# Attention laid out pair by pair: the odd row block's scores ahead of both weighted sums, turns and the layer norm's root in one fixed order

## What is computed

```python
x = x + attn(layernorm(x), Wqkv, bqkv, Wo, bo)
x = x + ffn(layernorm(x), gate_w, up_w, down_w, fc1_w, fc2_w, expert_w, ln_gamma, ln_beta)
# attn: 2048 rows in each of two sequences
qkv = x @ Wqkv + bqkv
p = softmax(q @ k.T / 16)
out = (p @ v) @ Wo + bo
```

## Time and profile before

| | us |
|---|---|
| median of 3 runs | 2429.43 (2427.39 to 2431.49) |
| the profiled execution | 2431.42 |
| its span, first to last instruction | 2429.6 |
| TensorE busy | 2324.2 (96%) |
| VectorE busy | 1762.6 (73%) |
| GpSimd busy | 1570.8 (65%) |
| ScalarE busy | 903.7 (37%) |
| transfers of the one queue | 382.38 MB, 54.1% of 16 engines' span |

### The profile page before, as it was taken

One profiled execution on the slowest core, in us unless ns is written; L12 is line 12 of the kernel. 1 busy time (PEld: TensorE's weight loads), 2 busy tenths in 40 slices (PEclk: granted clock), 3 DMA queues, 4 the chain that ended last, 5 costly groups with the idle time before them and its releaser, 6 DMA issues.

```text
span 2429.6 us, 31320 instructions
## 1 busy us (share of the span) xinstructions
PE 2324.2 (96%) x11224; PEld 1937.7 (80%) x11224; DVE 1762.6 (73%) x2952; ACT 903.7 (37%) x1695; POOL 1570.8 (65%) x1185
## 2 busy tenths in 40 slices
PE   6999999998999899999999999999999999999996
PEld 5888888887888788878887887787788778788875
DVE  6889957777777542954689775478795468977869
ACT  3222233333333352444432443443254343244442
POOL 4466525564555677499757469856749975744584
PEclk8999999999999999999999999999999999999998
DMA  8899845669566843344436343635534543633452
GB/s 219 251 314 303 256 151 174 193 200 314 169 199 194 242 130 95 101 120 129 117 106 183 107 129 90 150 93 161 146 103 119 130 113 101 190 105 98 120 155 91
DMA packets 218970, 386.48 MB, mean 159 GB/s; under 512 B 19648, under 2 KB 99648, under 8 KB 218176
## 3 DMA queue, kind: packets, MB, share of 16 engines
q1 hardware_dynamic: 217664, 382.38, 54.1%
q10 hardware_dynamic: 1152, 2.10, 0.2%
HBM read 260.67 MB, written 90.18 MB: 144 GB/s over the span
## 4 chain that ended last, share of the span: by engine, by line
PE 63%; DVE 12%; POOL 12%; DMA 6%; issue 3%; SPq 3%; ACT 1%; DVEq 0%; POOLq 0%; ACTq 0%
PE ps L2215 21%; PE ps L2216 20%; PE ps L2217 20%; POOL hq L2044 3%; DMA pland<-pturn 2%; POOL wr1l L1962 2%; POOL wr2l L1962 2%; POOL wr0l L1962 2%; SPq L637 2%; DVE xi L1292 2%; POOL pt L1962 1%; DVE pturn L1354 1%; DVE xr L1616 1%; POOL xr L2051 1%; DMA stf<-ups 1%
## 5 line engine op out<-in xcount | busy, mean ns | idle before, releaser
L1962 POOL TENSOR_TENSOR wr1l<-stf,wr1h 128x512 fp32r<-128x512 f32 x183 | 260.8, 1425 | 156.5 <-ACT wr1h L981 156.4
L1962 POOL TENSOR_TENSOR wr0l<-stf,wr0h 128x512 fp32r<-128x512 f32 x184 | 261.3, 1420 | 147.6 <-ACT wr0h L981 147.2
L1962 POOL TENSOR_TENSOR wr2l<-stf,wr2h 128x512 fp32r<-128x512 f32 x183 | 258.9, 1415 | 147.1 <-ACT wr2h L981 146.8
L1962 POOL TENSOR_TENSOR pt<-pland,pt 128x512 fp32r<-128x512 f32 x120 | 152.6, 1306 | 140.1 <-ACT pt L959 140.1
L981 ACT CAST wr1h<-stf 128x512 fp32r<-128x512 f32 x183 | 113.8, 622 | 313.5 <-PE ps L2217 252.2
L981 ACT CAST wr0h<-stf 128x512 fp32r<-128x512 f32 x184 | 114.4, 622 | 301.6 <-PE ps L2217 249.5
L981 ACT CAST wr2h<-stf 128x512 fp32r<-128x512 f32 x183 | 113.9, 622 | 298.8 <-PE ps L2217 246.9
L2215 PE MATMUL ps<-pt,vh 128*128 128x256 f32 x512 | 150.3, 294 | 28.0 <-POOL pt L1962 23.0
L1354 DVE STREAM_TRANSPOSE pturn<-prob 128x512 f32<-128x512 f32 x128 | 132.0, 1093 | 46.9 <-DMA pland<-pturn 39.9
L1234 DVE TENSOR_TENSOR hr2l<-hq,hr2h 128x512 fp32r<-128x512 f32 x78 | 95.1, 1219 | 90.4 <-ACT hr2h L1004 90.4
L1234 DVE TENSOR_TENSOR hr0l<-hq,hr0h 128x512 fp32r<-128x512 f32 x78 | 92.9, 1191 | 89.1 <-ACT hr0h L1004 89.1
(11 more groups left out here) (487 smaller groups left out, 7725.3 us busy)
## 6 DMA issues: line engine op xcount, KB each, us to landing
stf<-ups SPq DMA_DIRECT2D x160, 256.0 KB, 3.2
stf<-downs SPq DMA_DIRECT2D x160, 256.0 KB, 3.1
stf<-in_upw_dram SPq DMA_DIRECT2D x120, 256.0 KB, 2.7
pland<-pturn SPq DMA_DIRECT2D x112, 256.0 KB, 5.1
stf<-in_down_dram SPq DMA_DIRECT2D x88, 256.0 KB, 2.9
x<-in_x_dram SPq DMA_DIRECT2D x32, 512.0 KB, 5.9
x1d<-x SPq DMA_DIRECT2D x32, 512.0 KB, 3.3
xi<-in_x_dram SPq DMA_DIRECT2D x28, 512.0 KB, 9.7
```

What stands on the lines that cost most here:

```text
L1962: eng.tensor_tensor(lo, src, hi.bitcast(F32), ALU.subtract).then_inc(*done)
```

## The change

All five loops of the stage run over pairs C from 1 to 15 in place of blocks, with the exceptions of pair 8 kept in another form, and the end of the stage written out behind the loop.

TensorE: scores even, projection C - 2, scores odd, weighted sum (C - 1, 0), weighted sum (C - 1, 1). In pair 8 the projection comes first and the even sum stands between both scores. VectorE: maxima and turns of the even block, four residuals in one run, maxima of the odd block, all 15 steps of `ln2` in one run, turns of the odd block, both low parts of the weighted sum. ScalarE: exponentials even, parts of the previous odd block, exponentials odd, weighted sum 0, parts of the even block, weighted sum 1. GpSimd: low parts of the previous odd block, norm2, low parts of the even block, xadd. SyncE: shuffle even, store1, xload, qload, shuffle odd, store2. Keys 0 to 2 are loaded ahead of store1 of pair 7 and key block 3 behind its odd shuffle. The projection of pair 6 uses banks 6, 4, 5, 7 as most others do. The store of pair 13's normalized rows stands behind the shuffle of block 31 and the first weight fetches.

```diff
         def s_freed(g, kb):
-            return v_stt[(g - 3) // 2, kb] if g in (15, 31) and kb >= 2 else a_exp[g, kb]
+            return a_exp[g, kb]
         def wo_bank(C, u):
-            if C in (6, 14):
+            if C == 14:
...
+            for C in range(1, 17):
+                even, odd = 2 * C, 2 * C + 1
+                if C not in (8, 16):
+                    shuffle(even)
+                if C == 7:
+                    for kb in range(3):
+                        load_k(kb)
+                if C >= 2:
+                    store1(C - 2)
+                xload(C - 1)
+                if C == 8:
+                    shuffle(even)
+                    load_v(0)
+                if C == 15:
+                    w.wait_ge(*pt_lo(29, 3))
+                    for i in range(2):
+                        w.wait_ge(*d_x2[i][24 + i])
+                    load_x2(0, 0, 0, 4)
+                if C <= 13:
+                    w.wait_ge(*p_s[odd, 3])
+                    qload(C + 2)
+                if C < 16:
+                    shuffle(odd)
+                if C == 7:
+                    load_k(3)
+                if C == 8:
                     load_v(1)
...
+                if C == 15:
+                    for k in range(3):
+                        fetch(k)
+                if C == 16:
+                    fetch(3)
+                if C >= 2:
+                    for i in range(2):
+                        store2(C - 2, i)
+                if C == 16:
+                    fetch(4)
+                    fetch(5)
...
+            for C in range(1, 16):
+                even, odd = 2 * C, 2 * C + 1
+                if C == 8:
+                    pt_hi(even - 1)
+                    exps(even)
+                    at_hi(C - 1, 0)
+                    exps(odd)
                 else:
...
+                    exps(even)
+                    pt_hi(even - 1)
...
+                    exps(odd)
+                    at_hi(C - 1, 0)
+                pt_hi(even)
+                at_hi(C - 1, 1)
+            pt_hi(31)
...
+            for C in range(1, 16):
+                even, odd = 2 * C, 2 * C + 1
+                if C == 8:
+                    pt_low(15, 0)
+                    pt_low(15, 2)
                     for u in range(4):
...
+                        residual(C - 2, u)
+                maxima(even)
+                if C == 1:
+                    pt_low(1, 0)
+                    pt_low(1, 2)
+                turns(even)
+                if C >= 2 and C != 8:
                     for u in range(4):
...
+                        residual(C - 2, u)
+                if C == 8:
+                    at_low(C - 1, 0)
+                maxima(odd)
+                if C >= 2:
+                    ln2(C - 2, *range(15))
+                turns(odd)
+                if C != 8:
+                    at_low(C - 1, 0)
+                at_low(C - 1, 1)
...
-                elif C in (7, 15):
+                elif C == 15:
                     w.wait_ge(*v_at[C - 1, d])
...
+            for C in range(1, 16):
+                even, odd = 2 * C, 2 * C + 1
+                if C == 8:
+                    outputs(C - 2)
+                    scores(even)
+                    pv(C - 1, 0)
+                    scores(odd)
+                else:
+                    scores(even)
+                    if C >= 2:
+                        outputs(C - 2)
+                    scores(odd)
+                    pv(C - 1, 0)
+                pv(C - 1, 1)
+            outputs(14)
+            pv(15, 0)
+            pv(15, 1)
```

More of the change, by code:

```diff
@@ L1121, in _ @@
+            pt_hi(31)
+            w.wait_ge(*p_s[31, 3])
+            for j in range(4):
+                x_hi(0, 1, j)
+            at_hi(15, 0)
+            w_hi(0)
+            at_hi(15, 1)
+            w_hi(1)
+            w_hi(2)
             for n in range(NBK):
@@ new lines, in maxima, with turns @@
+            def maxima(g):
+                for kb in range(4):
+                    row_max(g, kb)
+                neg_max(g)
+            def turns(g):
+                for kb in range(4):
+                    turn_p(g, kb)
+                sums(g)
+            for C in range(1, 16):
[3 more added lines that the diff above has]
+                    pt_low(15, 2)
+                    for u in range(4):
+                        residual(C - 2, u)
+                maxima(even)
+                if C == 1:
+                    pt_low(1, 0)
+                    pt_low(1, 2)
+                turns(even)
+                if C >= 2 and C != 8:
+                    for u in range(4):
+                        residual(C - 2, u)
[8 more added lines that the diff above has]
+                at_low(C - 1, 1)
@@ L1801, in _ @@
+            w.wait_ge(*p_s[31, 3])
+            for j in range(4):
+                turn2(0, 0, j)
+            for u in (0, 2):
+                pt_low(31, u)
+            for u in range(4):
+                residual(14, u)
+            ln2(14, *range(15))
+            at_low(15, 0)
+            at_low(15, 1)
             for u in range(4):
@@ L2387, in up_mm @@
                 elif n == 0:
-                    w.wait_ge(*(a_exp[31, s] if s < 4 else v_stt[15, (0, 1, 3)[s - 4]]))
+                    w.wait_ge(*(a_exp[31, s] if s < 2 else v_stt[14, s] if s < 4 else v_stt[15, (0, 1, 3)[s - 4]]))
                 elif s < 3:
```

249 lines of the change are left out of this document (30 added, 219 removed).

## The result

| | before | after |
|---|---|---|
| median, us | 2428.41 (2425.14 to 2431.49) | 2408.91 (2407.86 to 2410.80) |
| profiled execution, us | 2431.42 | 2407.86 |
| its span, us | 2429.6 | 2406.0 |
| TensorE busy, us | 2324.2 | 2319.5 |
| VectorE, GpSimd busy, us | 1762.6, 1570.8 | 1747.8, 1569.9 |

The ratio of the medians is 0.9921, with a 95% interval of 0.9904 to 0.9938: 19.5 us faster, where 10.5 was forecast, and 2.1 us under the forecast's range of 2411 to 2437. The sign was right and so was what becomes of a settled pair; the size was not.

The account below looks back on a forecast made before the run. TensorE's waits in attention, 46 us of 476.2, were taken as the bound. Pairs of 27.9 put scores 30 18.4 us ahead, 10.5 surviving the end: 2431.4 - 10.5 = 2420.9 profiled, 2419.0 median; range 2411 to 2437.

Parts of the forecast that it names:

- settled pair: Attention pairs away from start, sequence turn and end: 27.9 us if nothing waits, against 30.44 and 30.26 us before.
- The bound and the mechanism: Attention: TensorE waits for the odd block's low parts; the new order gives that block 27.9 us instead of 16.7.
- The ring: VectorE's steps through the one buffer pturn: 27.75 us a pair with a 7.9 us shuffle, tying with TensorE's 27.9.
- Rival 1: The odd shuffle costs 9.4 us, ring 29.25, 1.4 us over TensorE in each of 14 pairs: 2438.6; chance 0.17.
- The residual: Settled pairs: the first residual's result, freeing the bank of weighted sum 0, comes 0.1 us before TensorE wants it.
- The start: First pairs: scores 3 wait 1.8 us; scores 4 start at 371.3, scores 6 at 400.3 after waiting for residual 0.
- (b): Sequence turn: key loads ahead of shuffle 15 at 315 GB/s; key block 3 lands about 560.5, scores 16 wait 5.3 us.
- (c): Sequence turn: residuals 6 run to 564, maxima 16 and the exponential to 567.8; scores 17 start at 569.8.
- Projection 6: Sequence turn: its input's low part stands on DVE behind turns 15, so it starts at 543.7, 3.9 us late.
- (d): Sequence turn: shuffle 17 behind 2 MB of value loads; residual (7,0) at 597.8, weighted sum (8,0) waits 0.4 us.
- The end: Projection 14 waits 4 us; pair 13's store delays block 31's parts to 798; 10.5 of 18.4 us survive.
- rival 3: Kind end: the store lands 6 us earlier and the middle gives 2 us less back: 2411; chance 0.15.

Follow-up runs that it names:

- The experiments on before: Kernel before with SyncE's even shuffle ahead of loads and stores, TensorE's odd scores ahead of both sums, or both edits: ratios 0.9994, 0.9990, 0.9912.
- ring_free: Changed kernel plus 15 single-input maxima over 4 columns on VectorE behind each root: 2444.30 us, ratio 1.0080.
- second trace: The changed kernel run once more, code unchanged: 2412.78 us, ratio 0.9936 to the kernel before.
- keys_small: Changed kernel loading only 128 of 1024 columns of each key block of the second sequence: 2409.88 us, ratio 0.9935 to the kernel before.
- store_ahead: Changed kernel with pair 13's store of normalized rows moved ahead of shuffle 31: 2409.52 us, ratio 0.9936 to the kernel before.
- in_place: Changed kernel with pair 13's normalized rows written over its residual, so block 31's parts wait for their shuffle alone: 2406.04 us, ratio 0.9919 to the kernel before.
- the two traces of before: The profiled kernel before and an unchanged repeat of it; the repeat measured 2424.37 us, ratio 0.9991 to the other runs of the same kernel.
- best: Changed kernel with pair 13's normalized rows written over its residual and pair 1 in the old order: 2402.74 us, ratio 0.9900 to the kernel before.
- ring_long: Changed kernel plus 15 small products with two SBUF operands on VectorE behind each root: 2572.81 us, ratio 1.0597.

## Why the prediction was too high

**The bound and the mechanism held.** TensorE's waits for the odd block's low parts went; the settled pair is 27.94 us between scores 6 and 14 and 28.11 between 20 and 30, against 27.9 forecast. Five pairs of 0.2 give the 1.0 us in the ledger. The experiments on before say more than the prediction did: it named the late even shuffle and the short cover of the odd block, without saying what either is worth alone; removing one of them is worth at most 3 us of the stage.

**The ring nearly tied, by two errors that cancel in part.** The shuffle takes 8.2 to 8.8 us from odd issue to even turn, not 7.9; the ring's other steps are 15.4 from an even issue to the odd one and 4.2 for the even turns, 19.5 or 19.6 and not 19.85. Rival 1 was to decide from a shuffle of 8.8 on, and the longest ones came to that edge (19.5 and 8.8 are 28.3, a pair of 27.9 and 0.4); at the mean the price was 0.2 us a pair. The residual that was to come 0.1 us early came 0.2 late at two settled sums. ring_free shows that the tie is real: 2.83 us more in the ring made the pair 2.7 to 3.4 longer. (GpSimd's 17.9 us a pair add up to 17.4 from the terms named; nothing hangs on it, since GpSimd idles 9.8 us.)

**The start.** Scores 3 waited 2.73 us in place of 1.8 and scores 4 came 1.1 us later than forecast (2.8 in the second trace); 1.1 of it came back in the next pair, which did not wait for residual 0 as I had it, so that scores 6 were on the forecast's date (1.6 late in the second trace). That they were on it in the first trace is two misses that cancel.

**The step that failed: (b) at the turn of the sequence.** Its mechanism was right and its size wrong. The forecast let the queue move 315 GB/s, from "some 3 MB" in 9.5 us of before, and so had shuffle 15 land 44 to 45 us after scores 14 and key block 3 at 48.6. ScalarE's parts of block 15, which wait for that shuffle, were released at 40.7 and 42.2 (548.11 and 549.59), and key block 3 was there at 44.75 (507.37 to 552.12; 43.3 in the second trace). Scores 16 waited 1.87 us (4.15 in the second trace) and not 5.3. The rate was too low because the bytes were an estimate: 360 GB/s were moved in that interval of before, and 377 to 409 in the 21 us of after. The same 8.19 MB would have taken 5.0 us more at 315 GB/s, of which 3.3 are the miscounted bytes (22.7 us at 360) and the rest a faster stretch of the queue. That this explains the date is worked out, not tested; keys_small shows that the loads carry weight there, 5.7 to 7.3 us in all. The Trainium skill (Perfetto Trace Analysis, Engine Utilization) gives about 435 GB/s as the ceiling of one core's 16 DMA engines; the windows lie under it, and the forecast's rate was 28% under it with nothing in the trace to say why.

The key block's date is 3.9 of the 4.8 us. Another 1.1 went from there to scores 17, for which the forecast had 9.3 us and the first trace took 8.2: 1.5 for the rest of scores 16, 5.9 for the weighted sum at a granted clock of 1.00 (553.6 to 559.5), and a wait of 0.79 for the exponential. In (c) the forecast had TensorE and not the exponential come last (569.8 against 567.8); in the second trace it was so, with no wait and a weighted sum of 6.6 us at a granted clock of 0.85. Projection 6 waited 3.08 us (1.34 in the second trace) and not 3.9; scores 16 waited for the key block behind it in any case. (d) held: weighted sum (8,0) waited 0.40 for residual (7,0), as forecast, and not at all in the second trace.

**The end.** Every date up to the store was right within 1 us: its issue was forecast 36.3 us after scores 30 and came at 36.4 (740.72 to 777.09), projection 14 was to wait 4 us and waited 3.1, the store and not the shuffle released the cast. Only the landing was shorter, 9.2 to 10.0 us in place of about 11, so the cast came 47.1 us after scores 30 and not 49. That is rival 3's mechanism at a third of its size. store_ahead and in_place show that the term was real: 3.1 and 7.2 us.

**The rest is open.** 465.6 less 4.8 in the middle and 1.8 at the end, plus 0.1 and 1.0 in the pairs, is the 460.15 us measured: a gain of 16.0 us in the stage, where 10.5 was forecast. The other 3.5 of the 19.5 us lie in no stage trace. The prediction carried the stage's gain to the median as exact, and the two traces of before alone differ by 8.3 us in code that the change doesn't touch. The stage's gain by itself would have left the time near 2412, inside the range; it took these 3.5 us on top to leave it. Why one execution's head and tail differ so much from another's (1953.4 and 1945.1 us for before, 1956.9 for best) no run here tells.

**Not settled.** Why best gained some 3 us more in the median than in_place while its trace shows no shorter stage (453.2 against 451.8) is open, too: the intervals (0.9883 to 0.9916 and 0.9903 to 0.9936) overlap.

## What to carry to other kernels

Where a product waits for the end of a chain through one buffer, look at both ends of the chain, the order of the queue that moves it and the order of the engine that feeds it: here either edit alone shortened the pairs and gave it back at the turn and the end, and both gave it all, so a failed first half is no verdict. Sum the ring through a single buffer as its own engine and keep the steps with two SBUF operands in a stretch where GpSimd waits for their result. Read the bytes of a queue from the trace and don't estimate them; and since a full queue moved anything from 304 to 413 GB/s here, give its rate a range, and carry that range through the sum. A gain read in one stage of one trace reaches the median only within the spread of the rest.

## What the runs showed of the hardware

- A two-operand step of VectorE on 128 x 2 numbers took 0.16 us with GpSimd idle, 0.85 in the mean and up to 1.2 with it busy on SBUF (ring_long); a one-operand reduction took 0.19 beside the same work (2.83 us for 15, ring_free). A one-operand TENSOR_SCALAR took 1.21 beside GpSimd, so the number of operands alone doesn't decide. Unexpected was how far this goes for tiny steps: 15 of them ran as long as GpSimd's ten instructions of 1.2 us beside them.
- The queue of one core, at a share of 0.99 or more, moved from 304 GB/s (before, 540 to 545) to 413 (before, 568 to 572), and 377 to 409 over 21 us of after, keys, shuffles, stores and loads mixed.
- Storing 1 MB of rows out of a strided tile landed in 9.2 to 10.0 us with shuffle 31 and three weight fetches ahead of it in the queue, 11.8 to 12.1 with 2 MB of loads ahead.
- Unchanged code of some 1950 us took from 1945 to 1957 us in the traces.
